# An attention and feed-forward sandwich on one core: reciprocal of the softmax sums first in VectorE's step, weight chunk over 16 steps, layer norms on ScalarE

## The reference

```python
x = x + _layernorm(attn(_layernorm(x), Wq, Wkv, Wkvh, Wg, Wout))
x = x + _layernorm(ffn(_layernorm(x), w_gate_up, w_proj))

def attn(x, Wq, Wkv, Wkvh, Wg, Wout):            # 16 heads of 128
    q, kv = x @ Wq.T, x @ Wkv.T
    kv_head = cumsum((x @ Wkvh.T) * exp(cumsum of log_sigmoid(x @ Wg.T)))
    kh, vh = kv_head[..., :16], kv_head[..., 16:]
    k, v = kp * kh per head, vp * vh per head    # kp, vp: halves of kv
    q, k = rope(q), rope(k)
    p = softmax(causal(q k' / sqrt(128)))
    return (p v, heads joined) @ Wout.T

def ffn(x, w_gate_up, w_proj):                   # hidden size 1024
    gate, up = split(x @ ternary_quant(w_gate_up).T)
    return rms_norm(silu(gate) * up) @ ternary_quant(w_proj).T
```

## Time and profile before

| what | value |
|---|---|
| median of 3 runs | 1160.51 us (1160.51 to 1162.78) |
| the profiled execution, its own time | 1161.09 us |
| its span, first to last instruction | 1159.3 us |
| TensorE's granted clock, mean | 0.99 of full speed |
| pair steps, roughly | 28 to 925 us of the span |
| feed-forward and drain | the rest |

### The profile page before, as it was taken

One profiled execution on the slowest core, in us unless ns is written; L12 is line 12 of the kernel. 1 busy time (PEld: TensorE's weight loads), 2 busy tenths in 40 slices (PEclk: granted clock), 3 DMA queues, 4 the chain that ended last, 5 costly groups with the idle time before them and its releaser, 6 DMA issues.

```text
span 1159.3 us, 26824 instructions
## 1 busy us (share of the span) xinstructions
PE 1076.3 (93%) x7990; PEld 1008.8 (87%) x7990; DVE 874.5 (75%) x2875; ACT 845.0 (73%) x2326; POOL 914.9 (79%) x845
## 2 busy tenths in 40 slices
PE   5799899989999999999899989999999899999996
PEld 4688898889888988898889888998988789999995
DVE  4578978897888779878987797878785656566563
ACT  2677777777777777787777777777777866666663
POOL 2687888797979797979798889888888647776774
PEclk8999999999999999999999999999999999999998
DMA  8260102010211111111011111111031000000000
GB/s 283 78 197 29 56 29 75 18 64 19 74 31 52 42 60 37 46 55 47 28 55 55 38 28 55 37 38 47 29 105 34 1 1 20 19 18 18 18 28 28
DMA packets 35192, 57.77 MB, mean 50 GB/s; under 512 B 3120, under 2 KB 15984, under 8 KB 34800
## 3 DMA queue, kind: packets, MB, share of 16 engines
q1 hardware_dynamic: 32912, 53.56, 14.9%
q10 hardware_dynamic: 2176, 3.15, 0.8%
HBM read 50.66 MB, written 9.18 MB: 52 GB/s over the span
## 4 chain that ended last, share of the span: by engine, by line
POOL 43%; issue 28%; PE 22%; ACT 3%; DVE 2%; DMA 1%; POOLq 1%; ACTq 0%; DVEq 0%; SPq 0%
POOL arena L526 13%; POOL arena L536 11%; POOL arena L547 9%; PE psum L835 8%; PE psum L852 6%; POOL arena L558 5%; PE psum L658 4%; POOL X L517 2%; ACT arena L1079 1%; PE psum L872 1%; POOL arena L503 1%; PE psum L753 1%; DVE pt_split L1318 1%; POOL arena L496 1%; PE psum L887 1%
## 5 line engine op out<-in xcount | busy, mean ns | idle before, releaser
L558 POOL TENSOR_TENSOR arena<-arena 128x768 f32<-128x768 f32 x128 | 188.2, 1470 | 106.7 <-DVE arena L1305 100.6
L526 POOL TENSOR_TENSOR arena<-arena,tables 128x512 f32<-128x512 f32 x128 | 174.4, 1363 | 17.5 <-ACT arena L979 17.5
L1318 DVE SCALAR_TENSOR_TENSOR pt_split<-psum,vh_col,pt_split 128x256 fp32r<-128x256 f32 (+1 forms) x512 | 187.3, 406 | 0.0
L753 PE MATMUL psum<-arena 128*128 128x256 f32 x512 | 157.6, 389 | 28.8 <-POOL arena L536 27.0
L536 POOL TENSOR_TENSOR arena<-arena 128x512 f32<-128x512 f32 x128 | 175.8, 1374 | 10.7 <-POOL arena L526 1.1
L990 ACT ACTIVATE arena<-arena 128x256 f32<-128x256 f32 x256 | 129.9, 507 | 74.4 <-DVE arena L1295 69.1
L547 POOL TENSOR_TENSOR arena<-arena 128x512 f32<-128x512 f32 x128 | 164.5, 1285 | 6.2 <-DMA arena<-kh_rows 6.2
L1280 DVE TENSOR_TENSOR arena<-psum,tables 128x512 f32<-128x512 f32 x128 | 86.1, 673 | 100.7 <-PE psum L658 95.2
L978 ACT ACTIVATE arena<-psum 64x512 f32<-64x512 f32 x128 | 76.1, 595 | 105.2 <-DVE arena L1280 105.1
L658 PE MATMUL psum<-wo_hi,o_hi 128*128 128x256 f32 x512 | 152.7, 298 | 0.0
L658 PE MATMUL psum<-xt_hi,wq_hi 128*128 128x256 f32 x512 | 146.9, 287 | 0.0
(11 more groups left out here) (161 smaller groups left out, 3511.5 us busy)
## 6 DMA issues: line engine op xcount, KB each, us to landing
arena<-kh_rows SPq DMA_DIRECT2D x128, 256.0 KB, 3.3
out<-spare SPq DMA_DIRECT2D x16, 256.0 KB, 2.1
arena<-w_rows SPq DMA_DIRECT2D x6, 512.0 KB, 4.3
X<-L_attn_Wout SPq DMA_DIRECT2D x1, 2048.0 KB, 14.8
X<-L_attn_x SPq DMA_DIRECT2D x1, 2048.0 KB, 9.5
w_rows<-L_ffn_w_gate_up ACTq DMA_DIRECT2D x4, 512.0 KB, 8.0
arena<-L_attn_Wq SPq DMA_DIRECT2D x1, 1536.0 KB, 10.4
X<-L_attn_x SPq DMA_DIRECT2D x1, 1536.0 KB, 15.7
```

The source lines that it names most:

```text
L526: nc.gpsimd.tensor_tensor(swap, swap, spread, ALU.mult).then_inc(q_sined, 1)
L558: nc.gpsimd.tensor_tensor(tb, tb, r.unsqueeze(3).to_broadcast([P, HP, 3, P]), ALU.mult).then_inc(p_ready, 1)
L753: nc.tensor.matmul(sj[:, 0:2 * P], q[:, j, P:N], kt[:, j, :], start=True, stop=True, skip_group_check=True)
L1318: last = nc.vector.scalar_tensor_tensor(pt_lo[p % 2][:, o], b[:, i], vh[:, t, h:h + 1], pt_hi[p % 2][:, o].bitcast(F32), ALU.mult, ALU.sub ...
```

## The change

- On VectorE `invert_sums` comes first in every step; statistics, keys' cosine and coefficients come behind it, ahead of the cosine multiply.
- The chunk's work is spread over 16 steps. Sum, scales, the first compare (`weights_above`), decision, change and finish stand behind the reciprocal; the second compare (`weights_below`) and the multiplication by the scale (`weights_sign`) stay at the end of their step. The second compare is a plain `is_lt` against a third scale, minus half.
- The two layer norms of the attention's batches are ScalarE activations with scale and bias, ahead of the swap in steps 1 and 7. VectorE makes the bias, minus mean times the inverse root, in one product of [128, 2] (`bias_x`, `bias_y`).
- GpSimd's `invert_x` moves behind the key scaling. The chunk is copied to another buffer in step 15 and stored from ScalarE's queue; SP's store and its wait are gone.

`bias_y` is like `bias_x`; semaphores and small tiles that are only declared are left out, and so is what moves without a change inside (`weights_sum`, `weights_change`).

```diff
-WSTEP = dict(load=0, cast=1, sum=2, compare=3, decide=3, change=5, finish=6, turn=7, copy=7, store=10, stored=12)
+WSTEP = dict(load=0, cast=0, sum=1, scale=2, above=3, below=3, decide=7, sign=7, change=9, finish=11, turn=15, copy=15)
...
-        w_bf, w_signs, w_other, w_tern = (carve(FF // 2).bitcast(BF16) for _ in range(4))
+        w_words = [carve(FF // 2) for _ in range(4)]
+        w_bf, w_signs, w_other, w_tern = (a.bitcast(BF16) for a in w_words)
...
-        w_turned_bf = w_stage[:, 0:FF // 2]
+        w_turned_bf = w_words[2]
...
-                    c0 = chunk_at(g0, par, s, "stored")
-                    if c0 is not None:
-                        sp.wait_ge(wt_stored, chunks_done(c0))
...
-                    c0 = chunk_at(g0, par, s, "store")
-                    if c0 is not None:
-                        rows = tern_flat[bass.ds(address(c0 * (P * FF // 2 // ROUND) - P * FF // 4), P * FF // 2)]
-                        sp.wait_ge(wt_copied, chunks_done(c0))
-                        sp.dma_start(rows.rearrange("(p f) -> p f", f=FF // 2), w_turned_bf).then_inc(wt_stored, 16)
                     if isinstance(g0, int) and g0 == STEPS - PAIRS and s == 0:
+                        sp.wait_ge(wt_stored, 16 + 16 * CHUNKS)
                         for c in range(CHUNKS):
                             sp.dma_start(w_final[c], tern_dram[c]).then_inc(wt_back, 16)
...
                     queries_add(g0, s)
-                    c0 = front_at(g0, s, "stats")
-                    if c0 is not None:
-                        invert_x(c0)
                     normalise(g0, s)
                     scale_keys(g0, par, s)
+                    c0 = front_at(g0, s, "stats")
+                    if c0 is not None:
+                        invert_x(c0)
                     c0 = tail_at(g0, s, "invert")
...
-                if not isinstance(c0, int) and not par:
-                    pe.wait_ge(wt_copied, c0)
+                if par:
+                    pe.wait_ge(wt_copied, min(c0 + PAIRS, ROUND + CHUNKS * ROUND) if isinstance(c0, int) else c0 + PAIRS)
...
+            def norm_x(c0):
+                xs = x_tiles(c0)
+                act.wait_ge(ln1_biased, c0 + PAIRS)
+                at_least(act, xt_turned, c0)
+                for t in range(NT):
+                    nc.scalar.activation(xn[:, t, :], xs[:, t, :], ACT.Identity, bias=ln1_bias[:, t:t + 1],
+                                         scale=ln1_rstd[:, t:t + 1]).then_inc(ln1_done, PAIRS // NT)
+            def norm_y(c0):
+                act.wait_ge(ln2_biased, c0 + PAIRS)
+                act.wait_ge(x1_done, c0 + PAIRS)
+                for t in range(NT):
+                    nc.scalar.activation(y_norm[:, t, :], y_sb[:, t, :], ACT.Identity, bias=ln2_bias[:, t:t + 1],
+                                         scale=ln2_rstd[:, t:t + 1]).then_inc(ln2_done, PAIRS // NT)
             def split_x(c0, par):
...
+                    at = act.snap(c0 * (P * FF // 2 // ROUND) - P * FF // 4)
+                    rows = tern_dram.rearrange("c p f -> (c p f)")[bass.ds(at, P * FF // 2)]
                     act.wait_ge(wt_turned, chunks_done(c0))
                     nc.scalar.activation(w_turned_bf.bitcast(BF16), F_BANK.bitcast(BF16), ACT.Copy).then_inc(wt_copied, ROUND)
+                    act.wait_ge(wt_copied, chunks_done(c0) + ROUND)
+                    act.dma_start(rows.rearrange("(p f) -> p f", f=FF // 2), w_turned_bf).then_inc(wt_stored, 16)
...
+                    c0 = front_at(g0, s, "norm")
+                    if c0 is not None:
+                        norm_x(c0)
+                    c0 = tail_at(g0, s, "norm")
+                    if c0 is not None:
+                        norm_y(c0)
                     swap(g0, s)
                     weights_place(g0, s)
...
             weight_hi(0)
+            norm_x(0)
             weight_hi(1)
...
-            nc.vector.memset(ones[:, :], 1.0)
+            nc.vector.memset(ones[:, :], 1.0).then_inc(wt_copied, ROUND)
+            nc.vector.memset(gate_mark, 0.0).then_inc(wt_stored, 16)
...
-            def norm_x(c0, par):
-                xs = x_tiles(c0)
+            def bias_x(c0):
                 dve.wait_ge(ln1_inv, c0 + PAIRS)
-                at_least(dve, xt_turned, c0)
-                for t in range(NT):
-                    nc.vector.scalar_tensor_tensor(xn[:, t, :], xs[:, t, :], ln1_agg[:, t, 0:1],
-                                                   ln1_rstd[:, t:t + 1].to_broadcast([P, E]), ALU.subtract, ALU.mult)\
-                        .then_inc(ln1_done, PAIRS // NT)
+                nc.vector.scalar_tensor_tensor(ln1_bias, ln1_agg[:, :, 0], -1.0, ln1_rstd, ALU.mult, ALU.mult)\
+                    .then_inc(ln1_biased, PAIRS)
             def split_x(c0, par):
                 dve.wait_ge(xt_hi_done, c0 + PAIRS)
...
+            def bias_y(c0):
...
+            def weights_scale(g0, par, s):
+                c0 = chunk_at(g0, par, s, "scale")
+                if c0 is not None:
                     dve.wait_ge(wt_summed, chunks_done(c0))
                     nc.vector.tensor_scalar(w_scale, w_sums, 1.0 / GROUP, 1e-8, ALU.mult, ALU.max).then_inc(wt_scaled, ROUND)
                     nc.vector.tensor_scalar(w_half, w_sums, 0.5 / GROUP, 0.5e-8, ALU.mult, ALU.max)\
                         .then_inc(wt_scaled, ROUND)
-            def weights_compare(g0, par, s):
...
+                    nc.vector.tensor_scalar(w_below, w_sums, -0.5 / GROUP, -0.5e-8, ALU.mult, ALU.min)\
+                        .then_inc(wt_scaled, ROUND)
...
-                    half = w_half.unsqueeze(2).to_broadcast([P, FF // GROUP, GROUP])
-                    dve.wait_ge(wt_scaled, chunks_done(c0, 2))
-                    nc.vector.tensor_tensor(heads(w_signs, GROUP), heads(w_bf, GROUP), half, ALU.is_gt)
-                    nc.vector.scalar_tensor_tensor(heads(w_other, GROUP), heads(w_bf, GROUP), -1.0, half, ALU.mult,
-                                                   ALU.is_gt).then_inc(wt_compared, ROUND)
+                    dve.wait_ge(wt_scaled, chunks_done(c0, 3))
+                    nc.vector.tensor_tensor(heads(w_signs, GROUP), heads(w_bf, GROUP), spread_groups(w_half), ALU.is_gt)\
+                        .then_inc(wt_above, ROUND)
+            def weights_below(g0, par, s):
+                c0 = chunk_at(g0, par, s, "below")
+                if c0 is not None:
+                    dve.wait_ge(wt_stored, chunks_done(c0))
+                    nc.vector.tensor_tensor(heads(w_other, GROUP), heads(w_bf, GROUP), spread_groups(w_below), ALU.is_lt)\
+                        .then_inc(wt_compared, ROUND)
             def weights_decide(g0, par, s):
                 c0 = chunk_at(g0, par, s, "decide")
                 if c0 is not None:
+                    dve.wait_ge(wt_above, chunks_done(c0))
                     dve.wait_ge(wt_compared, chunks_done(c0))
...
+            def weights_sign(g0, par, s):
+                c0 = chunk_at(g0, par, s, "sign")
+                if c0 is not None:
+                    dve.wait_ge(wt_decided, chunks_done(c0))
+                    nc.vector.tensor_tensor(heads(w_signs, GROUP), heads(w_signs, GROUP), spread_groups(w_scale), ALU.mult)\
+                        .then_inc(wt_signed, ROUND)
...
-                    spread = w_scale.unsqueeze(2).to_broadcast([P, FF // GROUP, GROUP])
-                    dve.wait_ge(wt_decided, chunks_done(c0))
-                    nc.vector.tensor_tensor(heads(w_signs, GROUP), heads(w_signs, GROUP), spread, ALU.mult)\
-                        .then_inc(wt_signed, ROUND)
...
-                    c0 = front_at(g0, s, "stats")
-                    if c0 is not None:
-                        stats_x(c0)
-                        gather_x(c0)
+                    invert_sums(g0, s)
+                    c0 = vh_at(g0, s)
+                    if c0 is not None:
+                        copy_vh(c0, par)
                     c0 = front_at(g0, s, "norm")
                     if c0 is not None:
-                        norm_x(c0, 1 - par)
-                    c0 = vh_at(g0, s)
-                    if c0 is not None:
-                        copy_vh(c0, par)
+                        bias_x(c0)
+                    c0 = tail_at(g0, s, "norm")
+                    if c0 is not None:
+                        bias_y(c0)
                     c0 = front_at(g0, s, "decay")
                     if c0 is not None:
                         keys_cos(c0)
...
                         coefs(c0)
                         weigh_kv(c0)
                         sum_kv(c0, 1 - par)
+                    c0 = front_at(g0, s, "stats")
+                    if c0 is not None:
+                        stats_x(c0)
+                        gather_x(c0)
                     c0 = tail_at(g0, s, "stats")
                     if c0 is not None:
                         stats_y(c0)
                         gather_y(c0)
-                    c0 = tail_at(g0, s, "norm")
-                    if c0 is not None:
```

(17 more changed lines are left out.)

37 lines of the change are left out of this document (19 added, 18 removed).

## The result

The changed kernel takes 1181.49 us, median of 4 runs (1180.44 to 1183.83), against 1160.8 us in the same calls: a ratio of 1.0177, 95% interval 1.0158 to 1.0196. It is 20.7 us slower, where 1133 was forecast: outside the range and with the other sign.

A forecast was written before the change was run, and what follows sets the result against it. TensorE was taken to set the plain step, VectorE the chunk batch's crowded steps. Six rounds -24.6, two full batches -2.6, the last -0.7, the start -0.5: -28.4 from 1161.09, so 1133 us; range 1115 to 1153.

The forecast's parts named there:

- Part 4: Turn and copy in step 15, cast in step 0, store on ScalarE's queue: 1.2 us lost, bounds 0 and 2.2.
- about 2.2: ScalarE's added work in step 15, in us: y norm 0.8 late, copy 1.02, DMA issue 0.36.
- the 1.2: Us taken as lost in a round's second batch, as a light step's gaps take some of 2.2.
- The 0.3 for the cast: Us by which the cast in step 0 was to show in a round's first batch.
- Part 3: Reciprocal first in VectorE's step: gain 0.4 us, from the last two steps of a batch.
- it comes when it did: Claim that VectorE's cosine multiply keeps its time, standing behind both idle gaps, while reciprocal and normalise come earlier.
- its pair stays at 13.79: Claim that step 5's pair keeps its 13.79 us, as decays and coefficients hold more than its gaps.
- Ports: Rival, chance 0.17: pieces behind the reciprocal wait for the normalise or hold it, 5.3 us a round, half counted: 1149 us.
- Part 2: Layer norms moved from VectorE to ScalarE: 0.9 us a batch gained, off the step of 7.59.
- -0.5: Us at the start, as the first norm no longer stands behind two splits on VectorE; bounds 0 to -1.
- Part 1: Weight chunk spread over 16 steps: each piece fits its gap of 1.07 or 1.35 us or misses by a tenth or two.
- ScalarE in the chain: Rival, chance 0.08: norms ahead of the swap delay sine, add and scores, each 0.8 us counting, 26 us: 1165 us.

The follow-up runs named there:

- e1: The changed kernel with ScalarE's six rounds written out instead of looped, so no branch back; store left in place: 1151.41 us.
- e3: The changed kernel with the chunk's store and the wait ahead of it back in SP's queue, ScalarE's branch kept: 1153.54 us.
- e13: The changed kernel with store on SP, VectorE's old order, GpSimd's root back, sign in step 9, change in step 10, earliest x norms on VectorE: 1138.98 us.
- e10: e3 with VectorE's front and tail work again ahead of the reciprocal and GpSimd's root for x again ahead of the normalise: 1142.31 us.
- e5: The kernel before with only the layer norms moved to ScalarE, in the old order: 1153.47 us.
- e4: The kernel before with only VectorE's order changed, the reciprocal first: 1189.03 us.
- e9: The kernel before with only the chunk's work spread over 16 steps, store in SP's queue, norms on VectorE, old order: 1146.49 us.
- e2: The changed kernel with the store cut to 8 of 512 words of each row, the rest a constant written at the start: 1183.73 us.
- e8: e3 with ScalarE again waiting for its own copy of the chunk right ahead of the branch, without a DMA issue: 1171.81 us.

## Why the prediction was wrong

**Part 4 is the step that failed.** It took the second batch's end as "about 2.2" us of instructions (norm, copy, issue), 1.2 of it lost. That step and the next grew by 4.0 and 2.2 us over before in the mean of four rounds. The issue took 0.34 and the copy 1.02, as read; what the sum lacked is what an own-result wait does ahead of a branch, 3.6 us idle, and the clock at half behind it. Taking out either the branch (e1) or the wait with the store (e3) gives back 30 and 28 us: this alone turns the sign. And before's trace shows the delay: its branch stands at 414.50, the next record of ScalarE's sequencer at 416.92, and the exponents' idle time is 1.44 to 1.48 us at five ends and 0.68 at the sixth. The prediction had no term for it. The code showed a wait in front of a loop's end, on an engine that stands in the chain; the upper bound of 2.2 was made from durations alone. Where the wait is gone the 1.2 was about right: step 15 of e13 takes 7.31 us, the same step of its clean batch 6.29. The 0.3 for the cast was 0.9 with the new order (step 0 of a round 7.86 in e3, 7.00 in its clean batch) and nothing with the old one (7.04 and 7.03 in e10).

**Part 3, "it comes when it did" and "its pair stays at 13.79", was wrong too.** The last two steps of a clean batch did come down, from 6.65 and 6.22 to 6.27 and 6.28, but not by the order: e5, with the norms alone, has 6.30 and 6.30, and e4, with the order alone, 6.91 and 6.26. What the order did is lengthen steps 3 and 4, where keys' cosine and coefficients now stand behind the reciprocal: 7.58 and 7.89 for 7.29 and 7.47, 0.7 a batch. The gap of 1.35 us was filled with work that starts together with the normalise and is held up beside it; e3 to e10 says 11 us for the whole new order, and e4 says 27 when the norms are on VectorE as well. Without the gap at the round's end this is about half of what parts e3's 1153.5 from the forecast of 1133.

**The rival Ports had the mechanism, not the places.** Groups of after (mean ns), with the decays' line and the x bias below (ns min/median/max):

```profile
L1405 DVE TENSOR_TENSOR arena<-arena 128x1024 bf16<-128x1024 bf16 x6 | 11.7, 1946 | 0.0
L1381 DVE TENSOR_TENSOR arena<-arena 128x1024 bf16<-128x1024 bf16 x6 | 7.4, 1227 | 0.0
L1413 DVE TENSOR_TENSOR arena<-arena 128x1024 bf16<-128x1024 bf16 x6 | 4.1, 678 | 0.0
```

```profile
L1234 DVE TENSOR_SCALAR arena<-arena x16: 271/1448/1450, 14.8 to 857.4; 32x256 f32<-32x256 f32 x16
L1216 DVE SCALAR_TENSOR_TENSOR arena<-arena x16: 151/672/1380, 6.1 to 837.2; 128x2 f32<-128x2 f32 x16
```

Compare and change behind the reciprocal (L1381, L1413) take what they take undisturbed: VectorE is there first and the normalise is held (at 338.26 it took 2.45 us for 1.47, the compare having started at 338.15). That is one of the signs Ports named. Instructions that start later lose instead: the decays' scaling, and the sign at a step's end, beside the sine, 1946 ns for 1.21 us. The product of two elements, put at "0.2 by size", takes 672 ns in the median. The decays' scaling has one input in SBUF. The Trainium skill (SBUF — State Buffer, "Who interferes with whom") says that this kind can enter a mode that contends with GpSimd as well, and that issue order decides who blocks; the trace agrees with contention, 1448 ns against 334; which mode the instruction ran in no run here shows.

**Part 2 had the sign right and the size wrong.** Step 0 of the clean batch came down from 7.49 to 7.00, 0.5 and not 0.9; the whole clean batch gains 0.5 (e5). TensorE's wait before the scores fell by 20 us, but in e3, without the branch's gap, its wait before the turns is 36.1 us for 18.0:

```profile
PE psum L774 <- DVE pt_split L1340: 36.1, 98, 1.7
```

A wait that goes isn't time that goes, if the next one is close behind. The "-0.5" at the start was +4.5 by the end of step 8 (88.12 for 83.64); with the norms alone (e5) it is +3.3 (86.91).

**Part 1 and most of Part 4's placing were right.** Against a clean batch of its own kernel the chunk batch was forecast 0.7 longer (53.6 for 52.9) and the second 1.6 (54.5 for 52.9). With the store in SP's queue and norms on VectorE (e9) they are 1.0 and 1.7 longer (54.65 and 55.38 for 53.69). In e13 they take 54.0 and 54.8 in the mean of four rounds, 0.8 and 1.6 over its clean batch, near the 53.6 and 54.5 of the sum, and the kernel 1.9% less than before.

**ScalarE in the chain** was the rival on the right side, with a chance of 0.08 and 1165. Its mechanism, each norm 0.8 late and counted, is not what happened: the y norm put a swap off by 0.7, which cost 0.4 in step 7.

## What to carry to other kernels

In this kernel each branch back of a loop keeps ScalarE's queue from going on for 2.3 to 2.9 us, and what hides it is the work issued ahead of the branch and the waits that the instruction behind it has anyway. So look in the trace for the branch and the next record behind it, compare with the last pass, which falls through, and do not take the name beside an idle time on trust: look when that instruction ended. Before a wait for the engine's own last result is put at the end of a loop's body, look whether anything covers the delay. The store on a queue nobody waits for avoided it here (e3); the same wait a step earlier was not run. Idle gaps of one engine are no free room when another engine's work starts at the same event and the two hold each other up; move pieces one by one, and sum the steps rather than one wait.

## What the runs showed of the hardware that was not expected

- Behind each of 65 branches back (13 kernels, five each) ScalarE's next sequencer record stands 2.3 to 2.9 us later; behind one not taken 0.04 us in after, e2 and e8. With work queued the branch is passed early and the instruction behind it was late by 0.9 (before) to 1.0 us (e3), behind a wait for the engine's own result by 2.6 (e8) to 3.5 (after).
- An idle time of TensorE of some 3.3 us (430.98 to 434.24) was followed by 10.3 us at half clock in all (433.40 to 443.70). A round end in e8 cost 1.84 us where the clock stayed and up to 4.75 where it fell; in after it costs some 5.5 us more than in e3 (27.3 us over the six rounds, five such ends).
- A VectorE product of two elements took up to 1380 ns, and a scaling of 32x256 elements 1448 instead of 334, behind the reciprocal, where the GpSimd normalise starts too.
